# Two gated layers on one core: the first batch in two channel halves, paired reciprocals, sums and gating moved to GpSimd, and a new order

## What is computed

```python
def cond(r, k, v, w, u, time_emb):            # called with k = v
    tf = sigmoid(sum(time_emb, -1))
    decay = exp(-exp(w)) * (0.5 + 0.5 * tf)
    ek = exp(minimum(k, 30)); ekv = ek * v
    nf, df = scan(a * decay + ekv), scan(b * decay + ek)        # forward in time
    nb, db = the same in reverse
    euk = exp(minimum(u + k, 30))
    num = nf + nb - ekv + euk * v
    den = df + db - ek + euk
    return sigmoid(r) * (num / maximum(den, 1e-8)) * (0.8 + 0.2 * tf)

def layer0_ffn(h):                            # 1024 tokens, 8 experts, 2 of them for each token
    # routing: top 2 of h @ router; a token's place in its expert is its rank (capacity 320)
    # experts: silu(gate) * up, width 176;   shared part: the same, width 704
    return routed(h) + shared(h)

def layer1_ffn(h):
    w = softmax(top2(h @ W_gate.T))           # the weights sum up to 1
    return relu(h @ W_up.T) @ W_down.T + sum(w) * (h @ W_expert)

x = x + layer0_ffn(cond(x, k, k, w0, u0, time_emb))
x = x + layer1_ffn(cond(x, k, k, w1, u1, time_emb))
```

## Time and profile before

| what | value |
|---|---|
| three runs | 178.53, 178.94, 180.38 us; median 178.94 us |
| profiled execution | 179.44 us, its span 177.7 us |
| busy in the span | PE 144.6, DVE 134.6, ACT 71.2, POOL 69.2 us |
| PE's first matmul | 20.92 us |
| granted TensorE clock, mean | 0.987 |

### The profile page before, as it was taken

One profiled execution on the slowest core, in us unless ns is written; L12 is line 12 of the kernel. 1 busy time (PEld: TensorE's weight loads), 2 busy tenths in 40 slices (PEclk: granted clock), 3 DMA queues, 4 the chain that ended last, 5 costly groups with the idle time before them and its releaser, 6 DMA issues.

```text
span 177.7 us, 2207 instructions
## 1 busy us (share of the span) xinstructions
PE 144.6 (81%) x666; PEld 117.6 (66%) x666; DVE 134.6 (76%) x293; ACT 71.2 (40%) x168; POOL 69.2 (39%) x83
## 2 busy tenths in 40 slices
PE   0000297799999969995999999899999977999992
PEld 0000285688898858883777877677788856878781
DVE  0899979999998996724499969967589434787624
ACT  3699374454053005223427534623633201232330
POOL 5388022732487770560050050050002577762130
PEclk9999999789999999999999999999999999999998
DMA  4999999995002320129702072012104033332111
GB/s 96 255 340 369 395 413 258 194 279 200 1 31 96 111 87 32 37 48 331 281 1 74 3 221 74 30 44 76 61 17 148 30 116 90 112 101 89 59 59 59
DMA packets 14843, 23.61 MB, mean 133 GB/s; under 512 B 1974, under 2 KB 10375, under 8 KB 14704
## 3 DMA queue, kind: packets, MB, share of 16 engines
q1 hardware_dynamic: 13296, 19.49, 35.1%
q0 software_dynamic: 1536, 3.99, 7.1%
HBM read 15.29 MB, written 8.39 MB: 133 GB/s over the span
## 4 chain that ended last, share of the span: by engine, by line
PE 40%; DVE 33%; issue 9%; DMA 7%; POOL 7%; ACT 2%; SPq 0%; DVEq 0%; POOLq 0%; ACTq 0%
PE hb L833 23%; PE dn L833 10%; DVE euk L647 9%; POOL ek L403 4%; DVE df L604 4%; DVE nf L604 3%; PE tp L847 3%; DVE euk L639 2%; DMA buf<-slots_in 2%; DMA ekv<-slots_out,get_at 2%; DMA cond_s<-cond 2%; POOL ekv L403 2%; PE tp L923 2%; PE dk L833 2%; DVE df L597 1%
## 5 line engine op out<-in xcount | busy, mean ns | idle before, releaser
L833 PE MATMUL hb<-xc,sup_s 128*128 128x256 f32 x176 | 43.1, 404 | 2.3 <-DVE hid L684 2.3
L833 PEld LDWEIGHTS hb<-xc,sup_s 128*128 128x128 f32 x176 | 35.3, 204 | 8.2 <-DVE hid L684 3.1
L492 ACT ACTIVATE gate_a<-hb 128x256 f32<-128x256 f32 (+3 forms) x40 | 16.1, 403 | 35.5 <-PE hb L833 28.3
L343 POOL TENSOR_TENSOR euv<-euv,nf 128x512 f32<-128x512 f32 x6 | 7.8, 1296 | 55.6 <-DVE nf L604 55.6
L833 PE MATMUL hb<-bufT,mup_s 128*112 128x320 f32 (+1 forms) x96 | 27.3, 434 | 1.0 <-issue 0.5
L647 DVE RECIPROCAL euk<-euk 128x256 f32<-128x256 f32 x16 | 26.8, 1714 | 0.0
L847 PE MATMUL tp<-turn,xc 128*128 128x136 f32 x32 | 5.5, 325 | 22.4 <-DVE xc L656 22.4
L833 PEld LDWEIGHTS hb<-bufT,mup_s 128*112 128x112 f32 (+1 forms) x96 | 17.1, 181 | 9.1 <-issue 1.7
L833 PE MATMUL dn<-mdn_s,hidm 112*128 112x256 f32 x96 | 22.1, 380 | 0.0
L833 PE MATMUL dn<-sdn_s,hid 128*128 128x256 f32 x96 | 21.7, 381 | 0.1
L355 POOL DMA_INDIRECT slots_in<-htok,put_at x16 | 16.3, 1019 | 10.2 <-DVE put_at L729 5.8
(11 more groups left out here) (107 smaller groups left out, 203.1 us busy)
## 6 DMA issues: line engine op xcount, KB each, us to landing
mup_s<-mup SPq DMA_DIRECT2D x4, 704.0 KB, 15.3
slots_in<-outb SPq DMA_DIRECT2D x10, 256.0 KB, 9.2
slots_out<-outb SPq DMA_DIRECT2D x8, 256.0 KB, 2.2
buf<-slots_in SPq DMA_DIRECT2D x4, 384.0 KB, 4.7
k<-k_cm SPq DMA_DIRECT2D x4, 256.0 KB, 3.8
xc<-x_cm SPq DMA_DIRECT2D x4, 256.0 KB, 8.3
sup_s<-sup SPq DMA_DIRECT2D x2, 512.0 KB, 8.7
xt<-x_tm SPq DMA_DIRECT2D x1, 1024.0 KB, 11.0
```

The lines of the kernel that those rows point to most:

```text
L343: nc.gpsimd.tensor_tensor(euv[:, n % 2], euv[:, n % 2], nf[:], ALU.add).then_inc(num_ready[n], 1)
L492: nc.scalar.activation(dst, src, ACT.Silu).then_inc(silu_ready, 1)
L833: return nc.tensor.matmul(dst, w, m, start=first, stop=last)
```

## The change

Head: the load of `wu_s` goes out from ACT's queue and not from SP's. The gate's sigmoid of the condition is written as a tanh (two DVE instructions fewer). For layer 0 the caps are taken ahead of the exponential, on POOL (`cap_k`, `cap_uk`), except for batch 3 (`cap_late`, on DVE). Batch 0 of layer 0 is done in two channel halves (`first_tile` on DVE, `first_half` on POOL, `first_products` on PE), with a reciprocal for each half. Its other steps stay what they are.

Gate of all other tiles: the denominator's sum is on POOL (`denominator`; its maximum too for tiles 5 and 7). One reciprocal of the product of both halves' denominators, and a product with the other half's, take the place of two reciprocals (`pair`, `rden`). For layer 0 POOL multiplies the numerator by the sigmoid (`gate_num`) and by `rden` (`hidden0`; in batch 3 DVE does that one). In layer 1 the factor `oscale` is taken out of the gate and put into the relu and the routing weights, which ACT makes for batches 1 and 2. Routing loses a cast and three instructions per round. The gathers of batches 0 and 1 go into `buf` and not into `ek`, and no longer wait for `q1_ready`. ACT loads its silu table ahead of the first transposes. `SPLIT` is 3, so that two more chunks come ahead of the experts, and the tables have new numbers.

Cut to its core:

```diff
-SPLIT = 1
-TURN_AT = (6, 9, 14)
+SPLIT = 3
+TURN_AT = (3, 11, 16)
-STEPS0 = (6, 0, 0, 3, 1, 0, 1, 1, 0, 2, 2, 1, 1, 0, 0, 0, 0, 0, 0)
+STEPS0 = (6, 3, 0, 1, 0, 0, 0, 2, 0, 3, 1, 0, 1, 1, 0, 0, 0, 0, 0)
-SPREAD = {0: 1, 1: 4, 10: 5, 11: 5, 14: 5, 15: 8}
-H0_ON_VECTOR = (0, 3)
+SPREAD = {0: 1, 1: 7, 11: 8, 13: 8, 15: 8}
+H0_ON_VECTOR = (3,)
+Q1_ON_VECTOR = (1, 2, 3)
+MAX_ON_VECTOR = (1, 2, 3, 4, 6)
+CAPPED_FIRST = 3
...
-        got = ek[:].rearrange("p b c t -> p (b c t)").rearrange("p (k n d) -> p k n d", k=2, n=TB * 2)
+        got = buf[:].rearrange("p q r d -> p (q r) d")[:, 0:8].rearrange("p (k n) d -> p k n d", k=2)
...
-            sp.dma_start(wu_s[:], wu).then_inc(ld_small, 16)
...
+            def cap_k(b):
+                pool.wait_ge(ld_k[b], 16)
+                nc.gpsimd.tensor_scalar(ek[:, b], k[:, b], 30.0, None, ALU.min).then_inc(k_capped, 1)
+
+            def cap_uk(b):
+                if b == 0:
+                    pool.wait_ge(ld_small, 16)
+                for c in range(CH):
+                    nc.gpsimd.tensor_scalar(euk[:, 0, b, c], k[:, b, c], wu_s[:, 2, c:c + 1], 30.0, ALU.add, ALU.min).then_inc(uk_capped, 1)
...
+            def first_half(c):
+                pool.wait_ge(euv_ready, 1)
+                pool.wait_ge(bwd_done, 2 * c + 1)
+                nc.gpsimd.tensor_tensor(euk[:, 0, 0, c], euk[:, 0, 0, c], df[:, c], ALU.add).then_inc(den_summed, 1)
+                pool.wait_ge(bwd_done, 2 * c + 2)
+                nc.gpsimd.tensor_tensor(euv[:, 0, c], euv[:, 0, c], nf[:, c], ALU.add).then_inc(num_ready[0], 1)
+                pool.wait_ge(num_ready[0], c + 1)
+                pool.wait_ge(gate_ready, 1)
+                nc.gpsimd.tensor_tensor(euv[:, 0, c], euv[:, 0, c], xc[:, 0, c], ALU.mult).then_inc(gated, 1)
+
+            def denominator(l, b):
+                n = l * B + b
+                pool.wait_ge(euv_ready, n + 1)
+                pool.wait_ge(bwd_done, 4 * n + CH)
+                nc.gpsimd.tensor_tensor(euk[:, l, b], euk[:, l, b], df[:], ALU.add).then_inc(den_summed, 1)
...
+            def gate_num(b):
                 pool.wait_ge(num_ready[b], 1)
                 pool.wait_ge(gate_ready, b + 1)
-                nc.gpsimd.tensor_tensor(xc[:, b], xc[:, b], euv[:, b % 2], ALU.mult).then_inc(h0_ready[b], 1)
+                nc.gpsimd.tensor_tensor(euv[:, b % 2], euv[:, b % 2], xc[:, b], ALU.mult).then_inc(gated, 1)
+
+            def hidden0(b):
+                pool.wait_ge(gated, tiles_done(b))
+                pool.wait_ge(rden_ready, tiles_done(b))
+                nc.gpsimd.tensor_tensor(xc[:, b], euv[:, b % 2], rden[:], ALU.mult).then_inc(h0_ready[b], 1)
...
+            cap_k(0)
+            cap_uk(0)
             values(0)
+            cap_k(1)
             bonus(0, 0)
+            first_half(0)
+            cap_uk(1)
+            cap_k(2)
+            first_half(1)
             values(1)
+            cap_uk(2)
             for b in range(B):
-                if b not in H0_ON_VECTOR:
+                if b >= 1:
+                    denominator(0, b)
                     numerator(0, b)
                     scatter_behind(4 * b)
-                    gate_h0(b)
+                    gate_num(b)
+                    if b not in H0_ON_VECTOR:
+                        hidden0(b)
                     scatter_behind(4 * b + 1)
...
             pool.wait_ge(written[1], 32 * (E // 2))
-            pool.wait_ge(q1_ready, B)
+            pool.wait_ge(btp_ready, 3 * (E // 2))
             pool.wait_ge(routed, 1)
             for b in range(B):
+                if b == 2:
+                    pool.wait_ge(q1_ready, B)
...
             exp_k(0)
-            exp_uk(0, 0)
+            exp_uk0(0)
             act.wait_ge(gain_ready, 1)
             scale_fwd(0, 0, 0)
+            scale_fwd(0, 0, 1)
+            gate_x(0)
             exp_k(1)
...
+            exp_uk0(2)
+            nc.scalar.activation(spare[:], zsum[:], ACT.Silu).then_inc(silu_loaded, 1)
...
+            if STEPS0[0] >= 1:
+                scale_fwd(0, 1, 0)
             turned(0)
+            if STEPS0[0] >= 2:
+                scale_fwd(0, 1, 1)
+            gate_x(1)
...
-                    for c in range(CH):
-                        nc.vector.reciprocal(eu[:, c], eu[:, c]).then_inc(den_ready, 1)
...
+                    after(tick(nc.vector.tensor_tensor(pair[:], eu[:, 0], eu[:, 1], ALU.mult)))
+                    after(tick(nc.vector.reciprocal(pair[:], pair[:])))
...
+                    nc.vector.tensor_tensor(rden[:], pair[:].unsqueeze(1).to_broadcast([P, CH, T]), eu[:, ::-1], ALU.mult).then_inc(rden_ready, 1)
```

More of the change, by code:

```diff
@@ L73, in adaln_ffn @@
         euv = sb("euv", [P, 2, CH, T])
+        pair = sb("pair", [P, T])
+        rden = sb("rden", [P, CH, T])
         htok = sb("htok", [P, NT, C])
@@ L719, in place @@
                 v.wait_ge(pos_ready, r + 1)
[L720 to L723 removed]
+                n = (b1 - b0) * TB
+                counts = tp[0][:, s.start * E:s.stop * E].rearrange("p (n e) -> p n e", e=E).unsqueeze(1).to_broadcast([P, 2, n, E])
+                after(tick(nc.vector.tensor_tensor(ohp[:, :, s], counts, oh[:, :, s], ALU.mult)))
                 after(tick(nc.vector.tensor_reduce(pos[:, :, s], ohp[:, :, s], AX.X, ALU.add)))
[L725 removed]
+                tick(nc.vector.scalar_tensor_tensor(out=slot[:, :, s], in0=idx8[:, s, 0:2].rearrange("p n j -> p j n"), scalar=float(CAP), in1=pos[:, :, s],
                                                     op0=ALU.mult, op1=ALU.add))
@@ L833, in mm, with first_products @@
                 return nc.tensor.matmul(dst, w, m, start=first, stop=last)
+            def first_products():
+                for c in range(CH):
+                    pe.wait_ge(h0_ready[0], c + 1)
+                    for i in range(TB):
+                        at = c * P
+                        last = nc.tensor.matmul(tp[i][:, at:at + P + E], xc[:, 0, c, i * P:(i + 1) * P], turn[:, c],
+                                                start=c == 0, stop=c == CH - 1, skip_group_check=True)
+                    if c == CH - 1:
+                        last.then_inc(htp_ready, 1)
+                    for u in range(3):
+                        if c == 0:
+                            pe.wait_ge(ld_sup[u // 2], 16)
+                        for half in range(2):
+                            at = u * CH * 2 * P + c * 2 * P + half * P
+                            last = nc.tensor.matmul(hb[u][:, half * T:half * T + T], sup_s[:, at:at + P], xc[:, 0, c],
+                                                    start=c == 0 and half == 0, stop=c == CH - 1, skip_group_check=True)
+                        if c == CH - 1:
+                            last.then_inc(up_ready, 1)
             def turn_rows(b):
@@ L898, in _ @@
             pe.wait_ge(ld_router, 32)
[L899 removed]
+            first_products()
             for u in range(nearly):
```

275 lines of the change are left out of this document (165 added, 110 removed).

## The result

The changed kernel took **186.7 us** (median of 4 runs, 185.29 to 187.15) against 178.86 for the kernel before beside it: ratio 1.040, 95% interval 1.035 to 1.045. It is slower by 4%. The forecast was 177.9 us and its range ended at 181. The profiled run took 185.29, the shortest of the four, span 183.6 against 177.7: the 5.9 us more of span are what follows. The medians lie 7.8 apart; the 2 us between the two differences are in no trace.

The account below looks back on a forecast made before the run. From 32.25 us the bound was PE's work plus its releases at three places, ahead of that DVE. Terms -1.6 - 0.4 - 0.5 - 0.3 + 1.8 = -1.0 took 179.44 to 178.4, the median 0.5 lower: 177.9 us, range 175.0 to 181.0.

Parts of the forecast that it names:

- unit price: Layer 0's caps on POOL: 0.7 us assumed for 512 columns, between DVE's 0.43 and POOL's product at 1.27.
- second start: PE begins turning batch 1 of layer 0: forecast at about 29.0 us, against 32.25 before, a gain of 3.2.
- Gain 1.6: Layer 0's scatters on POOL: the last four end at 75.6 us, against 77.17 before.
- order of the queue: Batch 1's head: ACT's last exponential waits for `cap_uk(2)` behind `values(1)`, then a 1.28 us table load; PE idles some 7 us.
- port wait: DVE waiting for a POOL product: 1.2 us charged per tile whose gate is on the path, 0.6 per half tile.
- second rival: Head: POOL becomes the bound, first scatter at about 59 us, scatters end 2.3 later than before; 181.8 us, chance 0.14.
- Low clock behind `turn_x1`: Start of layer 1: after a gap of about 5 us PE runs at clock 0.50, a loss of 1.8 us.
- first rival: Tail: the gap before layer 1 does not bring PE's clock down; 1.8 us less, 176.1 us, chance 0.20.
- Experts: PE's 0.46 us stand in the experts, behind DVE's reciprocals (3.35 us, now 1.65 in a row): gain 0.4 us.
- 0.3 at 159.35: PE's 0.35 us gap at 159.35 taken as gone, since DVE's part moves ahead with the gathers: gain 0.3 us.
- Gathers: Tail: gathers wait for the last store, about 137.9 us, not the gate at 138.39: gain 0.5 us.
- third rival: Head: batches 0 and 1 run faster, scatters start by 52 us and end 3 earlier; 176.5 or 174.7 us, chance 0.18.

Follow-up runs that it names:

- h3: The changed kernel with GpSimd's caps replaced by two-input sums in the same places, limit at 30 left out there: 191.52 us, ratio 1.003 to the kernel before.
- f2: The changed kernel with layer 0's limit at 30 left out in all four batches: 190.34 us, ratio 1.006 to the kernel before.
- e3: The kernel before with SPLIT = 3 (layer 1's plan and the fetch moved by two): 189.51 us, ratio 1.009 to the kernel before.

## Why the prediction was wrong

**The step that failed** is the unit price: "A POOL instruction with one tensor and a scalar doesn't occur. It lies between DVE's 0.43 and POOL's product, 1.27; I take 0.7 for 512 columns". It took 1.50 for one operation and 2.4 to 2.5, in two halves, for two. More than twice the value taken, and outside its bounds too: the upper bound rested on the idea that one tensor to read can't cost more than two. Six tiles' worth at 0.7 were 4.2 us, at the upper bound 7.6; they were 11.9. An error of that size, 7.7, builds up along the walk and stays: first matmul 17.05 (forecast 12.9, +4.1), second half 23.43 (17.4, +6.0), first scaled half ready at 28.2 (20.3, +7.9), second start 36.90 (29.0, +7.9), first scatter 62.46 (55.1, +7.4), first expert product 89.81 (82.2, +7.6). In the sum it is the term "Gain 1.6": measured, the scatters ended 5.9 later than before, and the first expert product came 6.0 later. h3 shows the cause: cheaper instructions in the same places, and PE's second start comes sooner by what they save.

**The order of the queue** was read rightly: that the last exponential waits for `cap_uk(2)` behind `values(1)`, that the table load then costs, and that PE then stands (10.15, forecast 7). With f2's zero price the second start is 30.28, still 1.3 later than the 29.0 forecast with caps: the chain of batches 0 and 1 was walked too fast even without them, so at least 1.3 of the 7.9 isn't the caps'. (Its steps from 46.4 to 52.5 add up to 52.8; that is small beside it.) The port wait was charged once per tile at 1.2 and at 0.6 for a half; batch 1 had 0.95 in the changed kernel, 2.0 in f2, each half about 0.5. By the Trainium skill (SBUF — State Buffer, section "SBUF: two separate sides") GpSimd and a VectorE instruction with two SBUF inputs or in its two-port mode lock each other out of a shared port for a whole instruction; the rows agree (0.42 becomes 1.37 beside a sum of GpSimd), and at batch 1 it cost 1 to 2 us here.

**The second rival** named the right mechanism, GpSimd as the bound, with its point, 56.7 for the first scatter. That decided: the scatters started at 62.46. It got 0.14 and 181.8 us, since it was priced at the same wrong upper bound. Its argument against ("POOL is busy 39% of the span") used an average over the span, where the head's queue was what mattered.

**The rest held.** Low clock behind `turn_x1`: forecast 1.8, measured 4.44 - 2.75 = 1.7, behind a stand of 3.73 (forecast about 5); the first rival falls. Experts: forecast 0.4 gained and 0.3 at 159.35, measured 0.7 gained in the experts, the gap in layer 1 shrank to 0.23. Gathers: forecast 0.5 gained; from that first shared chunk to the first gather 3.75 instead of 4.60, 0.85 gained. From the first expert product on the terms sum to +0.6, and the span shows -0.1. The clock's term e3 shows alone; whether the smaller ones held by more than luck, these runs can't tell. The third rival needed scatters by 52, and they came at 62.

**Where the gain of the change went.** Without the caps' price (h3, f2) the new order equals the kernel before, no better. It starts PE up to 2 us sooner at batch 1, with the same work left. But f2's first expert product, at 88.17, is 4.3 later than the first chip's 83.83: in between lie two chunks more (3.5 us) and a stand of 4.92 for `hot`, and the low clock comes back behind the experts (5.20 us for 12 records that take 2.75 at full clock). That part is argued from the rows and not shown. The stand follows one of ScalarE's (last section). On the first chip, where the changed kernel's trace has no such stand, f2 and h3 might do better; that wasn't measured.
